# Relational stage: VectorE weighs the gathered rows with softmax weights read from a PSUM bank of their own, and four banks for sums in place of five

## The reference

```
def _L1_gnn_ref(x, W, attn_src, attn_dst, edge_index, edge_type):
    h_all = jnp.einsum('nf,rof->rno', x, W).reshape(r, n, h, d)
    h_src = h_all[edge_type, src]
    h_dst = h_all[edge_type, dst]
    scores = jnp.einsum('ehd,hd->eh', h_src, attn_src) + jnp.einsum('ehd,hd->eh', h_dst, attn_dst)
    scores = jnp.where(scores > 0, scores, NEG_SLOPE * scores)
    amax = jnp.maximum(jax.ops.segment_max(scores, dst, num_segments=n), 0.0)
    w = jnp.exp(scores - amax[dst])
    denom = jax.ops.segment_sum(w, dst, num_segments=n) + 1e-12
    w = w / denom[dst]
    msg = h_src * w[..., None]
    out = jax.ops.segment_sum(msg, dst, num_segments=n)
    return out.reshape(n, h * d)
```

## Time and profile before

| | |
|---|---|
| median of 3 runs | 4278.35 us (4278.26 to 4278.49) |
| profiled execution | 4282.39 us, span of its instructions 4280.6 us |
| busy in the span | PE 82%, PEld 64%, DVE 66%, ACT 45%, POOL 56% |
| granted TensorE clock, mean | 0.884 |
| relational gathers L1844 | 880, the first at 2614.8 us, the last at 3769.6 us |
| weighs L2020 | 440, 298.1 us busy |
| sums L1947 (PE) | 1760 records, 608.0 us busy |
| adds L2014 (DVE) | 880, 366.5 us busy |

### The profile page before, as it was taken

The page is one execution under the profiler, slowest core; times in us unless marked ns, Lnnn a source line. Parts: engine busy times, 40 slices in busy tenths (PEclk is TensorE's granted clock), DMA queues, the critical chain, the costliest instruction groups (busy, mean ns, idle before and its releaser), DMA issues. The chain is left out here.

```text
span 4280.6 us, 67721 instructions
## 1 busy us (share of the span) xinstructions
PE 3496.8 (82%) x17983; PEld 2745.1 (64%) x17984; DVE 2823.3 (66%) x7798; ACT 1936.6 (45%) x5274; POOL 2379.3 (56%) x2470
## 2 busy tenths in 40 slices
PE   8788888888888899799989996777777777756693
PEld 4466666666666799799974444565665655545692
DVE  5599999999999555411112223888888887875456
ACT  2455555555555133233323335655655555536230
POOL 5477777777777154300012224777777777737441
PEclk9899999999999899899989997878888777765896
DMA  6577777777776311111114445555555555534446
GB/s 199 192 208 204 205 203 204 202 206 201 203 202 191 140 39 41 54 37 37 35 56 176 182 180 191 168 161 161 163 163 163 162 163 158 162 103 144 127 132 214
DMA packets 266461, 656.43 MB, mean 153 GB/s; under 512 B 52764, under 2 KB 140984, under 8 KB 250408
## 3 DMA queue, kind: packets, MB, share of 16 engines
q0 software_dynamic: 128768, 394.47, 32.5%
q1 hardware_dynamic: 130328, 251.92, 17.2%
q10 hardware_dynamic: 7056, 6.43, 0.4%
HBM read 521.34 MB, written 131.29 MB: 152 GB/s over the span
## 5 line engine op out<-in xcount | busy, mean ns | idle before, releaser
L278 POOL DMA_INDIRECT attn_KV<-kv_tab,attn_stage x880 | 937.0, 1065 | 279.6 <-issue 252.6
L1844 POOL DMA_INDIRECT rel_V<-h_tab,rel_stage x880 | 887.9, 1009 | 309.0 <-issue 240.1
L1947 PE MATMUL rel_SP<-rel_V,rel_OH 128*128 128x264 f32 x1760 | 608.0, 485 | 2.6 <-DVE node L2014 1.6
L379 PE MATMUL attn_QP<-node,attn_OHT 128*128 x1760 | 507.2, 414 | 12.0 <-issue 5.7
L391 PE MATMUL attn_SP<-attn_KV 128*128 128x264 f32 x1760 | 491.5, 405 | 24.8 <-DVE node L493 24.5
L1947 PEld LDWEIGHTS rel_SP<-rel_V,rel_OH 128*128 128x128 f32 x1760 | 379.5, 237 | 76.7 <-ACT rel_OH L1882 9.6
L391 PEld LDWEIGHTS attn_SP<-attn_KV 128*128 128x128 f32 x1760 | 343.0, 200 | 99.0 <-issue 43.0
L2014 DVE TENSOR_TENSOR node<-node,rel_SP 128x264 f32 x880 | 366.5, 416 | 55.4 <-PE rel_SP L1947 34.3
L379 PEld LDWEIGHTS attn_QP<-node,attn_OHT 128*128 128x128 f32 x1760 | 333.0, 202 | 62.6 <-issue 17.5
L1740 PE MATMUL pr_H<-WX,pr_YT 128*128 128x512 f32 x784 | 346.8, 595 | 0.0
L454 DVE TENSOR_TENSOR attn_KV<-attn_KV,attn_QP 128x512 f32<-128x512 f32 x440 | 298.1, 678 | 61.8 <-DMA attn_KV<-kv_tab,attn_stage 61.7
(11 more groups left out here) (393 smaller groups left out, 6763.6 us busy)
## 6 DMA issues: line engine op xcount, KB each, us to landing
rel_OHT<-dst_rows SPq DMA_DIRECT2D x55, 1024.0 KB, 6.0
h_tab<-pr_H SPq DMA_DIRECT2D x49, 1056.0 KB, 4.0
attn_KV<-kv_tab,attn_stage POOLq DMA_INDIRECT x880, 3.8
rel_V<-h_tab,rel_stage POOLq DMA_INDIRECT x880
pair_Y<-y SPq DMA_DIRECT2D x105, 130.0 KB, 2.1
kv_tab<-qkv_KV SPq DMA_DIRECT2D x49, 256.0 KB, 2.1
mix_Y<-y_out SPq DMA_DIRECT2D x49, 256.0 KB, 4.4
attn_runs<-runs SPq DMA_DIRECT2D x55, 192.0 KB
```

What stands on the lines that cost most here:

```text
L278: pool.indirect_dma_start(out=KV[:, i * IT + u, 0:2 * FEAT], out_offset=None, in_=d["kv_tab"][:, :], in_offset=bass.IndirectOffsetOnAxis(a ...
L379: mm = pe.matmul(QP[(2 * i + v) % BANKS][:, (u % 2) * FEAT:(u % 2 + 1) * FEAT], OHT[:, u, :], query(blks[v]), start=True, stop=True)
L1844: pool.indirect_dma_start(out=V[:, i * IT + u, :], out_offset=None, in_=d["h_tab"][:, :], in_offset=bass.IndirectOffsetOnAxis(ap=stage[:, ...
L1947: pe.matmul(SP[(c * IT + u) % SUMS][:, 0:NUMC], OH[:, j * IT + u, :], V[:, j * IT + u, :], start=True, stop=True).then_inc(s["sums"], 1)
```

## The change

The weights no longer share the bank `CH`: `W` gets a bank `WB` of its own. The eight banks of PSUM are all in use, so the sums lose one (`SUMS` 5 to 4). `weigh` reads its second operand from `WB` in place of from `V`. ACT's copy into `V` stays, since the sums need the weights as columns, and so does DVE's wait for it (`w_copied`) ahead of the first weigh of a group. PE gets a wait ahead of the turning of `EX`: all weighs of the group before must be done, since they read the same bank.

```diff
@@ -1755,7 +1755,7 @@
     PERIODS = G + 2
     RING = 3
     QUADS = IT // 4
-    SUMS = 5
+    SUMS = 4
     LEAD = 3
@@ -1788,7 +1788,9 @@
         CH = ctx.enter_context(nc.psum_tensor("rel_CH", [P, 512], F32))
         SP = [ctx.enter_context(nc.psum_tensor(f"rel_SP{i}", [P, 512], F32)) for i in range(SUMS)]
-        T, W = CH[:, 0:P], CH[:, P:2 * P]
+        WB = ctx.enter_context(nc.psum_tensor("rel_WB", [P, 512], F32))
+        T, W = CH[:, 0:P], WB[:, 0:P]
+        weights = W.rearrange("p (h s) -> p s h", s=IT)
@@ -1977,6 +1979,8 @@
                     if has(g, G):
                         pe.wait_ge(s["rows_f"], 3 * g + 3)
                         pe.wait_ge(s["exp"], g + 1)
+
+                        need(pe, s["weighted"], g * PAIRS)
                         pe.transpose(W, EX[:, :], m.ident[:, :]).then_inc(s["w_turned"], 1)
@@ -2017,7 +2021,7 @@
                         at = j * IT + 2 * v
                         rows = V[:, at:at + 2, 0:FEAT].rearrange("p s (a b) -> p s a b", b=DH)
-                        dve.tensor_tensor(rows, rows, V[:, at:at + 2, FEAT:NUMC].unsqueeze(3).to_broadcast([P, 2, HEADS, DH]),
+                        dve.tensor_tensor(rows, rows, weights[:, 2 * v:2 * v + 2, :].unsqueeze(3).to_broadcast([P, 2, HEADS, DH]),
                                           ALU.mult).then_inc(s["weighted"], 1)
```

## The result

| | before | changed |
|---|---|---|
| median | 4278.42 us (4278.26 to 4282.48) | 4222.48 us (4219.40 to 4227.09) |
| ratio | | 0.9872, 95% interval 0.986 to 0.9884 |
| profiled execution, span | 4280.6 us | 4217.6 us |
| relational gathers: busy, mean | 887.9 us, 1009 ns | 833.9 us, 948 ns |
| first to last gather's start | 1154.8 us | 1100.7 us |

The kernel is 55.9 us faster, 1.3%. 4233 was forecast, within 4221 to 4252. The span of the profiled execution is 63.0 us shorter. 54.1 of that lies between the first and the last relational gather. The other 9 lie ahead of the first gather, which started at 2605.7 in place of 2614.8 us. The stages there were not changed, so these 9 us say nothing on the change.

What follows compares the result with a forecast made beforehand. POOL, issuing gathers without a stop, was taken as the bound, with 55.4 us of stretching. The weighs' 45 us go and other parts cost nothing: median run 4278.35 - 45 = 4233 us, range 4221 to 4252.

Steps and rivals of the forecast that it cites:

- POOL decides the period, and its gathers are stretched by the weigh: Relational stage: POOL's 16 gathers set the 21.02 us period; stretching, mostly by weighs, adds 55.4 us over 880 gathers.
- It is the second SBUF input: Weigh (L2020): a DVE instruction with both inputs in SBUF holds a gather to its end, 1.34 against 0.94 us.
- Rival 1: Weigh: the stretch belongs to the weigh as such, its writing of `V`, and does not go away; 4278 us, chance 0.08.
- 45 of the 55.4 us go: Relational gathers: weighs cause 81% of the stretching by the square of durations, so 45 us go and 10 us remain.
- the six other instructions with two SBUF inputs: DVE's L2030, L2051, L2042, L2066, L2039 and L2073, 294 to 426 ns: claimed to keep stretching gathers by 10 us.
- my low end of 34 us: Relational gathers: the shifted rhythm hits one more other two-SBUF-input instruction each period, 11 us come back, 34 us are won.
- Gathers at a mean of 955 to 965 ns, the last near 3725 us: Expected profile of relational gathers L1844: mean 955 to 965 ns, median 946, few over 1.2 us, last gather near 3725.
- The weigh's own time does not change: Weigh on DVE: 512 elements take 672 ns with one PSUM operand, 678 with both in SBUF; no difference taken.
- PE's wait bites and is covered: PE's turning of `EX`: the new wait delays it about 0.45 us, covered with 1.5 us left; cost nothing.
- 1.1 us of slack on DVE, break-even at 0.14 us a weigh: DVE's 19.09 us turn against POOL's new 20.2 leaves 1.1 us; up to 0.14 us more per weigh costs nothing.
- rival 2: Weigh (L2020): the strided broadcast PSUM read makes it dearer and DVE the bound; at the upper bound 4410 us, chance 0.04.
- Rival 3: DVE's turn: waits for sums grow from 0.64 to 2.3 us a period, leaving 15 us gain, 4263 us; chance 0.06.

## Why the prediction was right, and where it was off

- *POOL decides the period, and its gathers are stretched by the weigh.* Shown. The gathers' busy time fell by 54.0 us and the stage by 54.1.
- *It is the second SBUF input.* Shown by the read alone (nothing without it), by another SBUF tile (no help), by half of the weighs (half of the stretching, though a third of the time), and by an extra instruction with one and with the other kind of input (6.2 us and nothing). Rival 1, that the stretch belongs to the weigh and its write, is out.
- *45 of the 55.4 us go.* This term of the sum was mis-sized: 54.0 went. I had left 10 us to the six other instructions with two SBUF inputs, by the square of their durations. What stayed is 833.9 - 880 x 0.946 = 1.4 us. The step that failed is "if a gather strikes anywhere, the chance of a hit grows with the length and so does the wait", for two reasons.
  - *The length that counts is not the profile's duration.* In the trace of after, a gather's point fell inside one of the six 80 times, and those gathers are only 2.2 us longer in all. L2070 (L2066 of before) shows why. Its duration is 0.35 us, seven gathers met it in its last 0.11 us, and each was held to its end within 7 ns. The twelve that came 0.20 us or more ahead of its end took at most 28 ns more than the shortest gather. The extra instructions hold for their last 0.18 us with 120 elements and 0.565 with 480. As an estimate from these two, what holds is 1.06 ns an element and some 0.06 us. That is about 0.60 us of a weigh but only 0.20 us of an instruction of 128 elements, whose duration is 0.29 to 0.42. With these lengths the square gives the six 9% of the 55.4 us and not 19%, 5 us and not 10.
  - *The fixed rhythm missed them, which is luck.* In the trace of before a gather met one of the six 36 times, where their durations would make it about 97 (2.2 us a period over 1.25 us, 55 times), and these gathers are 1.4 us longer. The shift did bring more meetings, 80, nearly one more in each period, as my low end of 34 us supposed. It cost 0.8 us and not 11.
- *Gathers at a mean of 955 to 965 ns, the last near 3725 us.* They came out at 948 ns and 3706 us, by the same term and, for the last gather, by the 9 us ahead of the first.
- *The weigh's own time does not change.* 672 ns where 678 stood. The nearest row, L1999 with 672, had it exactly.
- *PE's wait bites and is covered.* It bites by 0.54 us a period (0.45 forecast), and with it, and with four banks, the kernel took what the kernel before takes as long as the read stayed in SBUF.
- *1.1 us of slack on DVE, break-even at 0.14 us a weigh.* The wait for rows is 1.1 us as forecast, but the slack is larger. Three extra instructions, 1.7 us, cost nothing. That bound of rival 2 was too low, since waits inside DVE's turn give way too. Two small slips do not matter here: 98.5 us are 1.89 us in each of 52 periods (1.93 divides by the 51 waits), and half of rival 2's 0.04 is 0.02, so slower should have had 0.02 and not 0.03.
- *Rival 3, longer waits for sums.* They did not grow: 25.8 us, where 33.4 stood.

## What to carry to other kernels

Where GpSimd issues indirect DMAs one behind the other, look at the spread of their durations, not at the engines' busy shares: a median of 0.946 and a mean of 1.009 us was the whole gain here, and the timeline named the VectorE instruction that overlapped the long ones. Moving one of a VectorE instruction's two inputs from SBUF to PSUM was worth a bank where GpSimd was the bound and the bank was not missed. Where GpSimd waited for others, as on the slower chip, it won nothing. The long instructions come first: the weigh of 512 elements cost 54 us, the six of 128 and 256 together 1.4. An engine's slack can be larger than its wait for the rows, since waits inside its turn can give way: three extra instructions were free here. It is smaller than its period less its busy time: with six, DVE was busy for 977 of 1040 us and was the bound all the same.

## What the runs showed of the hardware

- A gather that met a VectorE instruction with two SBUF inputs was held to the end of it. In the trace of before, 172 gathers had their point in the last 0.60 us of a weigh (0.678 us). They were held for 47.7 us, of 48.0 us that those weighs had left. Of the 33 that came earlier in a weigh, 12 were held and 21 were not.
- An instruction with two SBUF inputs held gathers for less than the profile's duration: the last 0.18 of 0.268 us with 120 elements, the last 0.565 of 0.643 us with 480. A gather that came in the first 0.08 us passed.
- Some holds outlast one weigh. In the attention layer of the changed kernel 32 gathers took 1.85 us and more (median 0.948). One of them, with what it met:

```profile
610.18 0.67 DVE L454 TENSOR_TENSOR attn_KV<-attn_KV,attn_QP 128x512 f32<-128x512 f32 x1
...
610.40 1.88 POOL L278 DMA_INDIRECT attn_KV<-kv_tab,attn_stage  x1 [0.30 <-issue]
...
610.78 0.67 DVE L471 TENSOR_TENSOR attn_KV<-attn_KV 128x512 f32<-128x512 f32 x1
```

  Its point falls into an instruction that reads PSUM and SBUF, a weigh follows on it, and the hold ends with the weigh. Three gathers of the relational layer did the same in the run with all but the read (up to 1783 ns). With the attention weigh's second input in PSUM the longest was 1172. Other gathers with a weigh 0.39 us behind their start were not held. What makes the difference was not tested.
- The Trainium skill ("SBUF — State Buffer", "Who interferes with whom") reports a probe in which `tensor_tensor` did not stall DMAs, and gives as the inferred reason that descriptors need the write interface. For indirect DMAs these runs show otherwise: 54 us in 880 gathers came from `tensor_tensor` alone. Its rule on two SBUF inputs is what the trace shows. Which access of a gather is held, that to its row numbers in SBUF or another, no run separates.
- A strided and broadcast input from PSUM costs VectorE nothing more than one from SBUF: 669 and 680 ns for 512 elements, in the same execution.
